# A two-block convolution kernel: first half image loaded in two parts, stores moved, ScalarE reordered around the second norm

## Chip, cores and metric

One core of one Trainium2 chip. The time is device microseconds of one execution of the whole program. The engines run their own instruction streams: TensorE (PE), VectorE (DVE), ScalarE (ACT), GpSimd (POOL) and SyncE (SP), which here only issues DMAs.

## What is computed

Four images of 64x64 pixels with 16 channels pass through two blocks, all in float32:

```python
# block 0
h  = layernorm(x) @ w_te + b_te                      # 16 -> 32
F  = fft2(h); fr = concat(real(F), imag(F))
fc = gelu(fr @ w_fc + b_fc)
x1 = x + real(ifft2(fc)) @ w_tp + b_tp
h2 = layernorm(x1) @ w_fe + b_fe                     # the "second norm"
d  = gelu(depthwise_conv3x3(h2) + b_dw)
x2 = x1 + d @ w_fp + b_fp
# block 1
qkv = conv3x3(layernorm(x2) @ w_hidden, w_qkv)       # 192 outputs: q, k, v
o   = irfft2(rfft2(q) * rfft2(k)) on 8x8 patches
out = (v * layernorm(o)) @ w_out + x2
```

## The kernel before

The program is one block in which each engine has a hand-written order, tied together by semaphores. The four images form two groups g = 0, 1 of two images each (128 partitions = 2 images x 64 rows). A norm has a number k (0, 1, 2) and runs per group and half: `centre` and `spread` on VectorE, `square` on ScalarE (L588), `variance` on VectorE (L787), `deviation` (square root) on ScalarE (L593), `normalise` on VectorE (L792, L793). k = 1 is the norm ahead of the depthwise convolution, k = 2 the one ahead of block 1.

Depthwise stage: for each group TensorE transposes four `windows` (L1157) of zp into banks 0 to 3; an eviction `w_evac` (L339) brings each into `uw`; `depthwise(j)` is three matmuls, each of two instructions (L1175), into bank 4 + j % 4; ScalarE applies Gelu with the bias (L677); `project(j)` (L1183) writes bank j; VectorE adds to x1 (L881), which gives x2. j runs over 0 to 7, four per group. ScalarE loads another function table whenever it changes between square root and Gelu (`load_table`, L582), but plain copies go with either.

Between the blocks the normed x2 is transposed (`channel_major`, L1192), scaled into `tr` with a border (`bordered`, L807), and split into three bf16 parts in `tr9` (`part` on ScalarE, L602 and L605; `split` on VectorE, L800 and L802). SyncE stores both to scratch tensors in DRAM: `store_padded(b)` (L445, three DMAs) and `store_parts(b)` (L452, six DMAs; for image 0 the last three are issued by ScalarE, L674). It then loads them back shifted, as the image of 9 taps: `load_taps` (L463, float32, 128 rows x 8 slots, each 4 x 66 - 2 = 262 elements) and `load_last` (L472, the same in bf16, 524 B each); together they are a "chunk", half an image in six DMAs. There are eight chunks; `arena` has room for four, and a buffer of the second group's is loaded when its four steps n have been gathered.

Block 1 runs 32 steps n, four per chunk. VectorE (`gather`) and ScalarE (`gather9`), both L378, lay out two tiles; TensorE runs `conv(n)` (L1229, 12 recorded instructions) into banks 0 and 1, ScalarE copies it out (`conv_out`, L709), then come `forward(n-1)` (L1240), ScalarE's `k_out` (L716), VectorE's `product` (L916) and `inverse(n-2)` (L1250) into bank 4 or 5. `forward(m)` waits for `product(m-1)`. For steps 0 and 1 of this loop group 1's last norm and `channel_major(1)` are still to be done. `keep_warm(times, a, free)` (L996) issues matmuls whose result is not used, into bank `free`; each gives two recorded instructions.

At the end `turn_weighted` (L1274), for i = 14 and 15, waits for VectorE's scaling (L937) of each, then come the last two output projections `unit` (L1286).

## Time and profile before

| | us |
|---|---|
| median of 3 runs (lowest to highest) | 236.66 (236.47 to 239.24) |
| the profiled execution | 237.58 |
| its span | 235.8 |
| TensorE busy | 219.5 (93%) |
| VectorE busy | 159.4 (68%) |
| ScalarE busy | 133.8 (57%) |
| GpSimd busy | 76.9 (33%) |

The span runs from the first to the last recorded instruction; the rest of an execution's time lies around it. Of the chain of work that ended last, 68% is TensorE's, 16% VectorE's, 6% ScalarE's and 6% DMA's. The stages: up to about 44 us load, first norm and the spectral part, to 56 the inverse transforms, to 94 the depthwise stage, and from 100 the 32 steps of block 1. A group of a timeline merges neighbouring instructions of one kind; the time in brackets is the engine's idle time before them and what ended it. Matmuls are pipelined, so merged TensorE groups overlap a little.

### The profile page before, as it was taken

Reading aid. Unit: us, or ns where it says so; the run is one execution under the profiler, and the core shown is the slowest. Engines: PE = TensorE matmul, PEld = TensorE weight load, DVE = VectorE, ACT = ScalarE, POOL = GpSimd, SP = SyncE. Lnnn points to the kernel's source line nnn. Section 1 sums busy time; section 2 is a strip of 40 time slices with the busy share of each in tenths; the row PEclk is TensorE's granted clock in tenths of the full one; section 3 lists DMA queues with packets and bytes.
Section 4 is the critical chain, followed back from the end, with each engine's and each line's share of the span. In section 5 each row is a group of like instructions: output and inputs, shape, how many; then the busy total and the mean of one; then the engine's idle time right before and its main releaser. Section 6 shows DMA issues by size and latency. Waiting matters only on the chain.

```text
span 235.8 us, 4977 instructions
## 1 busy us (share of the span) xinstructions
PE 219.5 (93%) x1926; PEld 144.1 (61%) x1926; DVE 159.4 (68%) x301; ACT 133.8 (57%) x286; POOL 76.9 (33%) x70
## 2 busy tenths in 40 slices
PE   7989999895989899779999999999999999999983
PEld 3359434772447557268676676767676777767561
DVE  3995123567743983646489978678786889677793
ACT  3366475323174754344678666667667576766533
POOL 1635500012300000000051766426654364549730
PEclk9999999999799999999999999999999999999999
DMA  6920000000000018989997479999950000000001
GB/s 215 329 70 7 16 8 4 20 3 0 4 0 0 0 64 190 223 193 194 201 197 151 141 137 191 182 179 202 191 118 0 3 24 25 0 1 3 22 0 67
DMA packets 22647, 21.07 MB, mean 89 GB/s; under 512 B 1898, under 2 KB 21242, under 8 KB 22522
## 3 DMA queue, kind: packets, MB, share of 16 engines
q1 hardware_dynamic: 22352, 20.62, 43.0%
q8 instruction: 15, 0.25, 0.5%
q10 hardware_dynamic: 272, 0.14, 0.3%
q14 instruction: 8, 0.07, 0.1%
HBM read 16.58 MB, written 4.02 MB: 87 GB/s over the span
## 4 chain that ended last, share of the span: by engine, by line
PE 68%; DVE 16%; ACT 6%; DMA 6%; issue 2%; SPq 1%; DVEq 0%; ACTq 0%
PE psum L1229 22%; PE psum L1240 13%; PE psum L1250 7%; PE psum L1102 5%; PE psum L1175 4%; PE psum L1260 3%; DMA arena<-parts 3%; DVE xc L781 2%; PE psum L1080 2%; DVE sq L793 2%; PE psum L1090 2%; PE psum L1063 2%; DMA parts<-tr 2%; DVE st L787 2%; PE psum L1286 2%
## 5 line engine op out<-in xcount | busy, mean ns | idle before, releaser
L1229 PE MATMUL psum<-wc,tile 128*128 128x192 f32 (+1 forms) x384 | 59.4, 305 | 3.5 <-ACT tile L378 1.9
L1229 PEld LDWEIGHTS psum<-wc,tile 128*128 128x128 f32 (+1 forms) x384 | 51.4, 159 | 13.7 <-issue 7.8
L557 POOL TENSOR_TENSOR zp<-zp,ln 128x512 f32<-128x512 f32 x14 | 17.8, 1274 | 100.6 <-DVE zp L937 100.6
L916 DVE TENSOR_TENSOR arena<-psum,arena 128x512 f32<-128x512 f32 x32 | 22.1, 691 | 27.5 <-ACT arena L716 27.2
L378 DVE COPY tile<-arena 128x256 f32<-128x256 f32 x64 | 25.1, 435 | 2.1 <-DMA arena<-parts 2.1
L1175 PE MATMUL psum<-arena,wdw 102*128 102x512 f32 x48 | 23.5, 631 | 0.9 <-ACT arena L339 0.9
L716 ACT COPY arena<-psum 128x512 f32<-128x512 f32 x32 | 18.8, 586 | 9.0 <-PE psum L1240 9.0
L1250 PE MATMUL psum<-arena,km 128*64 128x256 f32 x128 | 20.9, 405 | 0.2 <-DVE arena L916 0.2
L709 ACT COPY spec<-psum 128x768 f32<-128x768 f32 x16 | 12.8, 799 | 12.7 <-PE psum L1229 12.7
L558 POOL TENSOR_TENSOR zp<-zp,ln 128x512 f32<-128x512 f32 x14 | 17.8, 1271 | 1.1
L1240 PE MATMUL psum<-spec,km 64*128 64x256 f32 x128 | 18.2, 402 | 0.0
L378 ACT COPY tile<-arena 128x128 f32<-128x128 f32 x64 | 16.7, 314 | 2.4 <-DMA arena<-parts 2.4
L588 ACT ACTIVATE sq<-xc 128x512 f32<-128x512 f32 x12 | 7.7, 640 | 14.6 <-DVE xc L781 14.6
L646 ACT ACTIVATE arena<-psum,wt 128x512 f32<-128x512 f32 (+1 forms) x20 | 10.6, 614 | 9.0 <-PE psum L1102 9.0
L1175 PEld LDWEIGHTS psum<-arena,wdw 102*128 102x128 f32 x48 | 8.8, 196 | 9.9 <-issue 9.1
L1240 PEld LDWEIGHTS psum<-spec,km 64*128 64x128 f32 x128 | 11.0, 186 | 3.2 <-issue 2.5
L1250 PEld LDWEIGHTS psum<-arena,km 128*64 128x64 f32 x128 | 6.3, 134 | 10.8 <-issue 10.1
L926 DVE SCALAR_TENSOR_TENSOR zp<-stat,psum 128x512 f32<-128x512 f32 x16 | 11.0, 687 | 1.7 <-DVE stat L920 0.5
L703 ACT COPY arena<-psum 128x512 f32<-128x512 f32 x16 | 9.4, 590 | 4.5 <-PE psum L1274 3.5
L996 PE MATMUL psum<-arena 128*128 128x512 f32 x16 | 10.4, 807 | 1.4 <-POOL arena L509 1.4
L832 DVE COPY spec<-psum 128x512 f32<-128x512 f32 (+1 forms) x5 | 3.0, 596 | 12.6 <-PE psum L1090 12.6
L937 DVE TENSOR_TENSOR zp<-zp,stat 128x512 f32<-128x512 f32 x16 | 11.1, 692 | 0.5
(129 smaller groups left out, 373.1 us busy)
## 6 DMA issues: line engine op xcount, KB each, us to landing
arena<-padded SPq DMA_DIRECT2D x16, 393.0 KB, 9.8
arena<-parts SPq DMA_DIRECT2D x16, 196.5 KB, 9.7
arena<-padded SPq DMA_DIRECT2D x8, 262.0 KB, 10.4
parts<-tr SPq DMA_DIRECT2D x12, 115.5 KB
wq<-w_qkv SPq DMA_DIRECT2D x1, 1296.0 KB, 11.9
padded<-tr SPq DMA_DIRECT2D x4, 264.0 KB, 3.9
arena<-parts SPq DMA_DIRECT2D x8, 131.0 KB, 9.6
out<-xt SPq DMA_DIRECT2D x8, 128.0 KB, 1.7
```

The costliest lines, as they stand in the source:

```text
L378: o = copy(dst[:, n % 2, 2 * h:2 * h + 2].rearrange("p a (q x y) -> p (a q) x y", q=2, x=8), a)
L557: pool_link(pool.tensor_tensor(y, y, along(0), ALU.mult))
L558: pool_link(pool.tensor_tensor(y, y, along(1), ALU.add))
L709: act.copy(qkv[n // 2 % 4][:, n % 2].rearrange("p (a t) c -> p a (t c)", a=2), psum[:, 0:1024].rearrange("p (a n) -> p a n", a=2)[:, :, 0: ...
L716: act.copy(kh[:, m % 2], f_half(m, 1)).then_inc(k_ev, 1)
L916: dve.tensor_tensor(pr[:, m % 2], f_half(m, 0), kh[:, m % 2], ALU.mult).then_inc(prod, 1)
L937: dve.tensor_tensor(y, y, per_group(s[:, 3, :]), ALU.mult).then_inc(signal, 1)
L1102: last = mm(mix_bank(n, turn)[:, 0:w], wmix1[rows, b].rearrange("p s n -> p (s n)"), sp[rows, spans(n)], start=(n > 0 and not again), stop ...
L1175: last = mm(bank[4 + t4][:, :], wdw[:, dy].rearrange("p x h -> p (x h)"), uw[0:KW, 4 * t4:4 * t4 + 4, 2 * g:2 * g + 2, dy:dy + S], start=( ...
L1229: last = mm(bank[a][:, HID * h:HID * h + HID], stationary[:, n % 2, 2 * h + a, :], moving[:, :], start=first and h == 0, stop=not first, s ...
L1240: last = mm(f_banks(m)[q][:, 256 * part:256 * part + 256], const(name)[rows], qkv[m // 2 % 4][rows, m % 2, :, CH * part:CH * part + CH], s ...
L1250: last = mm(o_bank(i)[64 * q:64 * q + 64, 256 * e:256 * e + 256], const("inv4"), pr[:, m % 2, q, :], start=True, stop=True)
```

## The change

In program order of the diff:

- the first chunk is loaded in two parts, of two tap rows t each (rows of 130 elements), with a semaphore `im_first` for the first; gathers n = 0 and n = 2 wait for a part each
- SyncE stores the padded form of both images of group 0 first, then its share of image 0's parts, and then loads; the stores of image 1's parts are issued by ScalarE, all six ahead of Gelu(7)
- ScalarE's order around norm 1: deviation of half 0 ahead of the square of half 1; one eviction instead of two ahead of each square of group 1; the Gelu table is loaded ahead of evictions 2 and 3
- variance, deviation and normalise of group 1 in norm 2 move behind the first gathers (n = 0 and n = 1), `bordered(1)` to n = 2, `channel_major(1)` behind `inverse(0)`
- conv(0) writes banks 4 and 5, waits for x2_done 6, and conv(1) no longer waits for its copy; inverse(0) waits for x2_done 8
- keep_warm gives four matmuls instead of five ahead of conv(0), and one instead of two at the end.

```diff
--- before.py
+++ after.py
@@ -296,6 +296,7 @@
         st_dma = [sem(f"st_dma{b}") for b in range(NB)]
         st9_dma = [sem(f"st9_dma{b}") for b in range(NB)]
         part_act, part_dve = sem("part_act"), sem("part_dve")
+        im_first = sem("im_first")
         im_ld = [[sem(f"im_ld{b2}{th}") for th in range(2)] for b2 in range(2)]
         tiled, qkv_mm, qkv_ev = sem("tiled"), sem("qkv_mm"), sem("qkv_ev")
         f_mm, k_ev, prod, o_mm = sem("f_mm"), sem("k_ev"), sem("prod"), sem("o_mm")
@@ -368,7 +369,11 @@
 
         def chunk_landed(engine, n):
             g, th, b2, _, _ = where(n)
-            if n % 4 == 0:
+            if n == 0:
+                engine.wait_ge(im_first, 16 * CHUNK_LOADS)
+            elif n == 2:
+                engine.wait_ge(im_ld[0][0], 16 * CHUNK_LOADS)
+            elif n % 4 == 0:
                 engine.wait_ge(im_ld[b2][th], 16 * CHUNK_LOADS * (g + 1))
 
         def gather_into(copy, dst, src, e, n):
@@ -391,6 +396,9 @@
 
         def o_bank(i):
             return bank[4 + i % 2]
+
+        def conv_base(n):
+            return 4 if n == 0 else 0
 
         def f_banks(m):
             return (bank[2], bank[3]) if m < 31 else (bank[0], bank[1])
@@ -452,8 +460,7 @@
                         sp_.dma_start(parts[b, s0 - 2:s1 - 2, i], tr9[C * lane:C * (lane + s1 - s0), b % 2, i, t0:t0 + 8, :]
                                       .rearrange("p t y -> p (t y)")).then_inc(st9_dma[b], 16)
 
-            def load_taps(b, th, done):
-                t0, t1 = 4 * th, 4 * th + 4
+            def load_taps(b, t0, t1, done):
                 at, w = S2 * t0, S2 * (t1 - t0) - 2
                 sp_.wait_ge(st_dma[b], 16 * PAD_STORES)
                 slots = padded.rearrange("s c b n -> (s c) b n")
@@ -462,8 +469,7 @@
                     src = bass.AP(padded.tensor, slots[0:1, b, dy + at:dy + at + w].offset, [[NB * 8 * S2, n], [C * NB * 8 * S2, 8], [1, w]])
                     sp_.dma_start(dst, src).then_inc(done, 16)
 
-            def load_last(b, th, done):
-                t0, t1 = 4 * th, 4 * th + 4
+            def load_last(b, t0, t1, done):
                 at, w = S2 * t0, S2 * (t1 - t0) - 2
                 sp_.wait_ge(st9_dma[b], 16 * PART_STORES)
                 rows = parts[b].rearrange("s i c n -> (i c) s n")
@@ -473,14 +479,15 @@
 
 
             def load_chunk(g, th, b2):
-                load_taps(2 * g + b2, th, im_ld[b2][th])
-                load_last(2 * g + b2, th, im_ld[b2][th])
-
-            store_padded(0)
+                load_taps(2 * g + b2, 4 * th, 4 * th + 4, im_ld[b2][th])
+                load_last(2 * g + b2, 4 * th, 4 * th + 4, im_ld[b2][th])
+
+            for b in range(2):
+                store_padded(b)
             store_parts(0)
-            load_chunk(0, 0, 0)
-            store_padded(1)
-            store_parts(1)
+            for p, done in enumerate((im_first, im_ld[0][0])):
+                load_taps(0, 2 * p, 2 * p + 2, done)
+                load_last(0, 2 * p, 2 * p + 2, done)
             sp_.wait_ge(fp_mm, 8)
             load_chunk(0, 0, 1)
             for b2 in range(2):
@@ -603,6 +610,13 @@
                 else:
                     act.wait_ge(part_dve, 4 * g + b2 + 1)
                     act.copy(part_of(1, b2), left_of(g, b2)).then_inc(part_act, 1)
+
+            def store_parts(b, lanes):
+                act.wait_ge(part_dve, parts_ready(b))
+                for s0, s1, lane, t0 in lanes:
+                    for i in range(3):
+                        act.dma_start(parts[b, s0 - 2:s1 - 2, i], tr9[C * lane:C * (lane + s1 - s0), b, i, t0:t0 + 8, :]
+                                      .rearrange("p t y -> p (t y)")).then_inc(st9_dma[b], 16)
 
             act.wait_ge(ready0, 2)
             load_table(ACT.Sqrt)
@@ -650,17 +664,22 @@
                     square(1, 0, (0,))
                 act.wait_ge(i1_mm, j + 1)
                 act.copy(yy[:, j].rearrange("p q x -> p (q x)"), bank[j][:, :]).then_inc(i1_act, 1)
+            deviation(1, 0, (0,))
             square(1, 0, (1,))
-            deviation(1, 0)
+            deviation(1, 0, (1,))
             act.wait_ge(m2_mm, 5)
             for h in range(2):
-                for j in (2 * h, 2 * h + 1):
-                    act.wait_ge(w_mm, j + 1)
-                    w_evac(act.copy, j).then_inc(w_act, 1)
+                act.wait_ge(w_mm, h + 1)
+                w_evac(act.copy, h).then_inc(w_act, 1)
                 square(1, 1, (h,))
             deviation(1, 1)
+            load_table(ACT.Gelu)
+            for j in (2, 3):
+                act.wait_ge(w_mm, j + 1)
+                w_evac(act.copy, j).then_inc(w_act, 1)
             for g in range(G2):
-                load_table(ACT.Gelu)
+                if g == 1:
+                    load_table(ACT.Gelu)
                 for j in range(4 * g, 4 * g + 4):
                     if j == 5:
                         part(0, 0, 0)
@@ -668,11 +687,9 @@
                         part(0, 1, 0)
                     if j == 6:
                         part(0, 1, 1)
-                        s0, s1, lane, t0 = LANES[1]
-                        act.wait_ge(part_dve, parts_ready(0))
-                        for i in range(3):
-                            act.dma_start(parts[0, s0 - 2:s1 - 2, i], tr9[C * lane:C * (lane + s1 - s0), 0, i, t0:t0 + 8, :]
-                                          .rearrange("p t y -> p (t y)")).then_inc(st9_dma[0], 16)
+                        store_parts(0, LANES[1:])
+                    if j == 7:
+                        store_parts(1, LANES)
                     act.wait_ge(dw_mm, j + 1)
                     act.activation(gd_of(j), bank[4 + j % 4][:, :].rearrange("p (t b y) -> p t b y", t=4, b=2),
                                    ACT.Gelu, bias=vec("b_dw")).then_inc(gelu2, 1)
@@ -683,7 +700,8 @@
                         act.wait_ge(w_mm, j + 1)
                         w_evac(act.copy, j).then_inc(w_act, 1)
                 square(2, g, (1,))
-                deviation(2, g)
+                if g == 0:
+                    deviation(2, 0)
 
 
             def gather9(n):
@@ -707,7 +725,7 @@
                 if n >= 8:
                     act.wait_ge(gated, n // 2 - 3)
                 act.copy(qkv[n // 2 % 4][:, n % 2].rearrange("p (a t) c -> p a (t c)", a=2),
-                         psum[:, 0:1024].rearrange("p (a n) -> p a n", a=2)[:, :, 0:2 * HID]).then_inc(qkv_ev, 1)
+                         psum[:, 512 * conv_base(n):512 * conv_base(n) + 1024].rearrange("p (a n) -> p a n", a=2)[:, :, 0:2 * HID]).then_inc(qkv_ev, 1)
 
             def k_out(m):
                 act.wait_ge(f_mm, m + 1)
@@ -740,6 +758,8 @@
                 if n % 2 == 0 and n >= 8:
                     turned((n - 8) // 2)
                 conv_out(n)
+                if n == 0:
+                    deviation(2, 1)
                 if n >= 1:
                     k_out(n - 1)
                 if n % 2 == 0 and n >= 4:
@@ -883,8 +903,8 @@
                     if j % 2 == 1:
                         dve.wait_ge(x2_done, j + 1)
                         centre(g, t4 // 2, x2)
-                variance(2, g)
                 if g == 0:
+                    variance(2, 0)
                     normalise(2, 0, xc[:, 0])
                     dve.wait_ge(tr_zero, 1)
                     bordered(0)
@@ -956,12 +976,14 @@
                 if n + 1 < 32:
                     gather(n + 1)
                 if n == 0:
+                    variance(2, 1)
+                if n == 1:
                     normalise(2, 1, xc[:, 1])
                 if n % 2 == 1 and n >= 5:
                     o_scale((n - 5) // 2, o_norm)
                 if n >= 1:
                     product(n - 1)
-                if n == 1:
+                if n == 2:
                     bordered(1)
                 if n % 2 == 0 and n >= 4:
                     o_variance((n - 4) // 2)
@@ -1212,7 +1234,7 @@
             depthwise(7)
             for j in range(5, 8):
                 project(j)
-            keep_warm(5, km, 2)
+            keep_warm(4, km, 2)
 
 
             pe.wait_ge(tr_ev, 2)
@@ -1221,12 +1243,14 @@
             def conv(n):
                 pe.wait_ge(tiled, n + 1)
                 pe.wait_ge(tiled9, n + 1)
-                if n >= 1:
+                if n == 0:
+                    pe.wait_ge(x2_done, 6)
+                if n >= 2:
                     pe.wait_ge(qkv_ev, n)
                 for first, stationary, moving in ((True, tile, wc), (False, tile9_bf, wc9)):
                     for a in range(2):
                         for h in range(2):
-                            last = mm(bank[a][:, HID * h:HID * h + HID], stationary[:, n % 2, 2 * h + a, :], moving[:, :],
+                            last = mm(bank[conv_base(n) + a][:, HID * h:HID * h + HID], stationary[:, n % 2, 2 * h + a, :], moving[:, :],
                                       start=first and h == 0, stop=not first, skip_group_check=True)
                 last.then_inc(qkv_mm, 1)
 
@@ -1244,6 +1268,8 @@
             def inverse(m):
                 i, e = divmod(m, 2)
                 pe.wait_ge(prod, m + 1)
+                if m == 0:
+                    pe.wait_ge(x2_done, 8)
                 if e == 0 and i >= 2:
                     pe.wait_ge(o_centred, i - 1)
                 for q in range(2):
@@ -1290,11 +1316,10 @@
                 conv(n)
                 if n >= 1:
                     forward(n - 1)
-                if n == 1:
-                    pe.wait_ge(x2_done, 8)
-                    channel_major(1)
                 if n >= 2:
                     inverse(n - 2)
+                if n == 2:
+                    channel_major(1)
                 if n % 2 == 1 and 7 <= n < 31:
                     turn((n - 7) // 2)
                 u = unit_after((n - 8) // 2)
@@ -1308,7 +1333,7 @@
             turn(13)
             turn_bias(14)
             turn_bias(15)
-            keep_warm(2, km, 3)
+            keep_warm(1, km, 3)
             turn_weighted(14)
             turn_weighted(15)
             unit(6)
```

## Rows read from the trace of the kernel before

**Rows 1.** Windows: length, busy us of PE, PEld, DVE, ACT, POOL, then PEclk, DMA, GB/s

```profile
58.30:61.70 3.40, 3.40 (x5) 1.30 (x6) 3.30 (x6) 0.00 (x0) 0.91 (x1) 0.54 0.03 7
...
150.00:235.80 85.80, 81.04 (x596) 56.67 (x596) 64.53 (x128) 52.87 (x116) 43.62 (x34) 1.00 0.35 65
```

**Rows 2.** Timeline of ScalarE, second norm: start, busy, instruction [idle before]

```profile
55.12 0.30 ACT L593 ACTIVATE st<-st,eps 128x32 f32<-128x32 f32 x1
...
57.46 0.58 ACT L339 COPY arena<-psum 96x512 f32<-96x512 f32 x1
...
68.20 1.28 ACT L582 ACT_TABLE_LOAD   x1
```

**Rows 3.** Timeline of VectorE around the second norm

```profile
53.87 0.68 DVE L781 SCALAR_TENSOR_TENSOR xc<-st,x 128x512 f32<-128x512 f32 x1
...
55.91 0.69 DVE L793 TENSOR_TENSOR zp<-xc,st 128x512 f32<-128x512 f32 x1
...
62.07 0.69 DVE L781 SCALAR_TENSOR_TENSOR xc<-st,x 128x512 f32<-128x512 f32 x1
```

**Rows 4.** Timeline of TensorE in the depthwise stage

```profile
58.30 3.46 PE L1175 MATMUL psum<-arena,wdw 102*128 102x512 f32 x4 [0.93 <-ACT arena L339]
...
70.33 1.13 PE L1183 MATMUL psum<-wt,arena 128*128 128x96 f32 x8 [0.98 <-ACT arena L677]
...
71.30 2.77 PE L1175 MATMUL psum<-arena,wdw 102*128 102x512 f32 x6
```

**Rows 5.** Timeline of SyncE's DMA queue around the first loads

```profile
89.39 2.07 SPq L463 DMA_DIRECT2D arena<-padded  x3
...
92.80 1.33 SPq L472 DMA_DIRECT2D arena<-parts  x3
```

**Rows 6.** Timeline of VectorE before and at the first gathers

```profile
95.84 0.69 DVE L781 SCALAR_TENSOR_TENSOR xc<-st,x 128x512 f32<-128x512 f32 x1
...
99.73 0.90 DVE L378 COPY tile<-arena 128x256 f32<-128x256 f32 x4 [1.81 <-DMA arena<-parts]
...
111.59 0.50 DVE L378 COPY tile<-arena 128x256 f32<-128x256 f32 x2 [0.25 <-DMA arena<-parts]
```

**Rows 7.** Timeline of TensorE from the warm matmuls to conv(4)

```profile
94.14 4.48 PE L996 MATMUL psum<-km 128*128 128x512 f32 x10
...
100.48 1.87 PE L1229 MATMUL psum<-wc,tile 128*128 128x192 f32 x12 [1.86 <-ACT tile L378]
...
103.33 1.87 PE L1229 MATMUL psum<-wc,tile 128*128 128x192 f32 x12 [0.98 <-ACT spec L709]
...
113.97 1.90 PE L1229 MATMUL psum<-wc,tile 128*128 128x192 f32 x12
```

**Rows 8.** DMA packets in 93:94, 97:98, 112:113 us; then two windows

```profile
DMA packets 226, 0.23 MB, mean 227 GB/s; under 512 B 9, under 2 KB 226, under 8 KB 226
...
DMA packets 430, 0.22 MB, mean 221 GB/s; under 512 B 20, under 2 KB 426, under 8 KB 430
...
DMA packets 154, 0.15 MB, mean 151 GB/s; under 512 B 10, under 2 KB 154, under 8 KB 154
...
90.70:99.20 8.50, 7.92 (x37) 4.70 (x35) 5.13 (x9) 4.04 (x7) 0.00 (x0) 1.00 1.09 225
...
95.00:105.00 10.00, 7.16 (x33) 4.54 (x31) 5.96 (x15) 3.49 (x11) 0.00 (x0) 1.00 0.96 203
```

**Rows 9.** Issues of two lines on two queues: durations ns min/median/max

```profile
L452 SPq DMA_DIRECT2D parts<-tr x21: 407/749/877, 86.9 to 137.0; - x21
...
L674 ACTq DMA_DIRECT2D parts<-tr x3: 319/438/442, 86.9 to 87.7; - x3
```

**Rows 10.** Timeline of ScalarE, the last Gelu of the depthwise stage

```profile
91.69 0.69 ACT L677 ACTIVATE arena<-psum,wt 128x512 f32<-128x512 f32 x1 [2.78 <-PE psum L1175]
```

**Rows 11.** Timelines of TensorE and VectorE at the end

```profile
227.24 1.88 PE L996 MATMUL psum<-km 128*128 128x512 f32 x4
...
229.00 0.69 DVE L937 TENSOR_TENSOR zp<-zp,stat 128x512 f32<-128x512 f32 x1
```

## The prediction

> **What bounds the kernel now.** I read the chain of work that ended last first, then the timelines of TensorE, ScalarE, VectorE and SyncE around each place the diff touches, then the windows and the DMA traffic. From 150 us to the end TensorE is busy 81.0 of 85.8 us and most of what is missing lies in the last microseconds [rows 1], so a microsecond won before that comes through to the end, and one won on another engine doesn't. TensorE stood still where the diff works: 0.93 us before the first depthwise matmul, 0.98 us before the first projection [rows 4], 1.86 us before conv(0) and 0.98 us before conv(1) [rows 7]. All times below are in the coordinates of the profile of before; what an earlier stage wins is added at the end. The profiled execution has a span of 235.8 us and a time of 237.58; the median of the runs is 236.66. I take the gain off the median.
>
> **Part A, ScalarE around the second norm.** Before, deviation(1,0,first half) ran at 55.12, behind a square that waits for the centring at 53.87 to 54.55 [rows 2, 3], although its variance was ready at 53.9. Moved ahead it ends at about 54.3 and VectorE can normalise as soon as the centring ends: reciprocal from 54.6, product from 54.97 in place of 55.91 [rows 3], 0.94 us earlier. The second half follows: its deviation ends at 56.6, and the first eviction (L339) behind it starts at 56.6 and not 57.46 [rows 2], so the first depthwise matmul starts at 57.4 and not 58.30 [rows 4]. TensorE has only four short transposes (L1157) to do in between, which fit.
>
> The second gain is the table load. Before, ScalarE did evictions 2 and 3, the last square, two deviations, and only then the Gelu table (68.20) [rows 2] and the first Gelu (L677), for which TensorE waited 0.98 us [rows 4]. Now the last square follows the centring of 62.07 to 62.76 [rows 3], which is 0.94 earlier, so ends at 62.5; the variances and deviations end at 63.4; the table load of 1.28 us and its small activation end at 65.0; evictions 2 and 3 run to 65.5 and 66.0, the first Gelu to 66.7. Depthwise(2) now waits for eviction 2, that is 65.5, and takes 2.65 us (depthwise(3), six matmuls, filled 71.30 to 73.9 [rows 4]), to 68.2. The projection starts there in place of 70.33: **2.1 us**. From 70.3 to 94.1 TensorE has no long idle time before and keeps its order, so the whole stage moves.
>
> The granted clock was 0.54 between 58.30 and 61.70 [rows 1], the lower of the two levels, 1.2 GHz, for most of it, and it fell just after the wait of 0.93 us [rows 4]. Four depthwise matmuls took 3.46 us there [rows 4], of which full clock would give back half. With the clock up depthwise(2) would still wait for eviction 2 at 65.5, with the clock down TensorE arrives at 65.6. So I count nothing for the clock: 2.1 us either way, bounds 1.7 and 2.2. The Trainium skill ("TensorE: Matmul & The Clock Gate", Part 1) says that K is binary, full or half rate; the trace agrees, and its 0.54 is a mix of the two.
>
> **Part B, the first half image.** Before: load_taps(0) is issued at 89.39, its last-tap loads at 92.80 because they wait for the stores of the parts [rows 5], and all has landed when VectorE starts its first gather at 99.73 [rows 6]; conv(0) follows at 100.48 [rows 7]. A chunk is 1024 rows of 1048 B and 1024 of 524 B, 1.61 MB. Rows of 1048 B went at 226 packets per us (227 GB/s), rows of 524 B at 430 (221 GB/s) [rows 8]: bytes bound both. All data together, padded(1)'s store among it, ran at 225 GB/s between 90.7 and 99.2; later, with slow heads of a load in it (154 packets per us), at 203 from 95 to 105 [rows 8]. I use 213 between them.
>
> After: the first part is 1024 rows of 520 B and 1024 of 260 B, 0.80 MB. At 213 GB/s that is 3.75 us. No row shows packets of 260 B in number. Lower bound: the same byte rate, 1.2 us for 1024. Upper bound of the nearest row: the same 430 packets per us as 524 B, 2.4 us. I take the middle, 0.6 us over the byte rate, for the sum and keep both ends. Ahead of them now run the stores of parts(1), six DMAs of 0.40 MB on ScalarE's queue, 1.85 us at the same rate. So: 90.7 + 1.85 + 3.75 + 0.6 + 0.5 (last data to landing, as 99.2 to 99.7) = 97.4. The loads of the last taps can't be issued before 92.8 either (their store is where it was; the second padded store is issued while SyncE waited for part_dve anyway), and the data of the taps and of parts(1) fills the time until 95, so this wait is covered. VectorE is free at 96.53 [rows 6], since variance(2,1) now comes behind the gathers; TensorE's four warm matmuls of 0.9 us end at 97.7 in place of five at 98.6 [rows 7]. So the load ends last: conv(0) at 97.4 + 0.75 = 98.15 (before: 99.73 to 100.48). Bounds 97.8 (warm matmuls) and 99.3.
>
> ScalarE's six issues come before Gelu(7). They start at 88.9, and by SyncE's median 0.75 us for a large one and ScalarE's 0.44 for a small one [rows 9] take 3 x 0.75 + 3 x 0.44 = 3.6 us, to 92.5. Gelu(7) was at 91.69 [rows 10], so it is 0.9 us late. Cover: TensorE is busy with projections 5 and 6 until 93.25 (the warm matmuls start at 94.14 [rows 7] and project(7) before them takes 0.9), and Gelu(7) ends at 93.2. Without that cover every microsecond more delays project(7), the warm matmuls and VectorE's last x2.
>
> Conv(1) has banks of its own and no wait for the copy of conv(0): its 0.98 us of idle goes [rows 7]. From conv(0) to conv(4) before were 113.97 - 100.48 = 13.5 us [rows 7], now 12.5: conv(4) at 110.65. Two things are late next. Part two of the chunk lands at 96.9 + 3.75 + 0.6 + 0.5 = 101.75, and conv(2), due at 98.15 + 4.75 = 102.9, needs 0.75 for its gathers: 0.4 us to spare. Behind this gather on VectorE lie normalise(2,1) (2.0 us) and product(0) (0.7), for which forward(1) waits; they end at 104.9, when it is due at 104.7: 0.1 to 0.2 us lost. And the second chunk (image 1), before ready at 111.59 [rows 6]: it wins 1.6 us (0.33 MB of padded(1) are stored earlier, in idle DMA time), about 1.0 us of the half-empty time behind the old stores, and loses up to 2.4 us for short rows, so 109 to 111.4, and conv(4) wants it at 110.0. Part B: 113.97 - 110.75 = **3.2 us**, bounds 1.7 and 3.6.
>
> The other moves (variance, deviation and normalise of group 1, channel_major(1) behind inverse(0)) shift the same instructions into gaps of VectorE's waits for DMA and k; the waits for x2_done 6 and 8 were met by 95.1. At nothing.
>
> **Part C, the end.** One warm matmul pair instead of two leaves at 228.3, not 229.1. The first turn can start then, the second waits for VectorE's last scaling, 229.00 + 0.69 [rows 11], and takes 0.9 us, to 230.6 in place of 230.9: **0.3 us**, bounds 0 and 0.3.
>
> **Sum.** 2.1 + 3.2 + 0.3 = 5.6 us; 236.66 - 5.6 = 231.1. The bounds together: 3.4 to 6.1, 230.5 to 233.3.
>
> **Rivals.**
> 1. Short rows cost twice. The sum has 1.85 us for 1024 rows of 260 B (1.25 by bytes and 0.6). If they took 4.8 us, half the rate of the 524 B rows, each part would land 2.95 us later: part two at 107.65, conv(2) at 108.4, conv(4) 12.5 - 4.75 = 7.75 us later at 116.15, 2.2 later than before. 2.1 - 2.2 + 0.3 = 0.2, time 236.5. For it: the trace has no such rows; against it: 524 B rows lost nothing against 1048 B. Chance 0.10. The Trainium skill ("DMA: Bandwidth & Descriptors", Specifications) gives 512 B as the least transfer for line rate, with a read-modify-write below; that speaks against this change, and by it the time would be this rival's 236.5; no run so far shows it.
> 2. The other side: the short rows go at the lowest packet rate of the trace, 154 per us [rows 8], 6.6 us for 1024. Twice 4.75 us more puts part two at 111.25, conv(2) at 112.0 and conv(4) at 119.75, 5.8 later than before; with 2.1 and 0.3 won the kernel would be 3.4 us slower, 240.1. The sign turns at conv(4) at 116.4, about 4.9 us per 1024 rows. Against it: those 154 are a short dip at the head of each load. Chance 0.03.
> 3. ScalarE is held by its issues, 1 us each (SyncE's longest was 0.88 [rows 9]), while SyncE issues too. Gelu(7) ends at 95.6, project(7) at 96.5, the four warm matmuls at 100.1, conv(0) at 100.2 and conv(4) at 112.7: Part B shrinks to 1.3, time 233.0. Chance 0.12.
> 4. Part A gives only its first 0.9 us, because an eviction or a deviation stands in the new order behind something late (the table load before evictions 2 and 3, above all). 0.9 + 3.2 + 0.3 = 4.4, time 232.3. Chance 0.13.
> 5. The change does not act: the first part is only ready when the whole was, as the stores of parts(1) and the second part share the engines with it. Then 0.98 + 2.1 + 0.3 remain, 233.3. Chance 0.08.
>
> **Numbers.** My forecast, with 229.7 to 232.6 around it, has 0.54. A measurement of this kernel can tell about 2%, here 4.7 us: under 231.9. The centre of the forecast is 0.8 past it. 0.44 of the forecast's 0.54, 0.05 of rival 4's 0.13 (its own spread reaches below) and 0.06 of rivals 3 and 5 lie there: faster 0.55; slower 0.02 (240.1 is not yet over 2%, the worst of rival 2 is); within 2% the rest, 0.43. The range for 8 in 10 is 229.6 to 234.8: it takes in rivals 3, 4 and 5 and leaves out 1 and 2.
>
> **What would show it.** First depthwise matmul 0.9 us earlier, the wait of L1183 for ScalarE gone and a short one of L1175 for L339 instead, project(0) at 68.2. Then, less 2.1: first gather at 97.4, four warm matmuls and under 1 us idle before conv(0), none before conv(1), conv(4) at 110.7. Wrong if TensorE waits for project(7), if packets under 512 B go at well under 400 per us, or if conv(2) or conv(4) waits for a gather over 0.5 us.

## The result, and the profile after

| | before | after |
|---|---|---|
| median of 20 runs each (lowest to highest) | 237.44 (235.69 to 240.12) | 235.64 (234.57 to 238.93) |
| ratio | 1 | 0.9932 (0.9903 to 0.996) |
| the profiled execution | 237.58 | 236.54 |
| its span | 235.8 | 234.7 |
| its mean granted clock | 0.993 | 1.0 |

The kernel is 0.7% faster by the ratio, 1.6 us, and 1.8 us by the medians, where 5.6 us were forecast; 235.64 lies outside the range of 229.6 to 234.8. The two spans differ by 1.1 us. Ratios, here and below, leave out executions over 1.5% above the fastest of their kernel, medians do not, so the two can differ.

The first group below is TensorE's timeline of the kernel after (start us, busy us, instruction, idle before and what ended it). It answers to [rows 4, 7, 11].

```profile
53.86 1.96 PE L1163 MATMUL psum<-arena,km 128*128 128x512 f32 x4 [0.80 <-ACT arena L666]
...
57.96 1.96 PE L1197 MATMUL psum<-arena,wdw 102*128 102x512 f32 x4 [0.93 <-ACT arena L340]
...
66.21 2.84 PE L1197 MATMUL psum<-arena,wdw 102*128 102x512 f32 x6 [0.92 <-ACT arena L340]
68.89 1.03 PE L1205 MATMUL psum<-wt,arena 128*128 128x96 f32 x8
...
92.77 1.13 PE L1205 MATMUL psum<-wt,arena 128*128 128x96 f32 x8 [0.91 <-ACT arena L694]
93.74 3.62 PE L1018 MATMUL psum<-km 128*128 128x512 f32 x8
99.07 3.53 PE L1253 MATMUL psum<-wc,tile 128*128 128x192 f32 x24 [1.71 <-ACT tile L383]
...
104.32 1.87 PE L1253 MATMUL psum<-wc,tile 128*128 128x192 f32 x12 [0.66 <-ACT spec L727]
...
112.92 1.87 PE L1253 MATMUL psum<-wc,tile 128*128 128x192 f32 x12 [0.73 <-ACT spec L727]
...
228.67 1.16 PE L1300 MATMUL psum<-km,zp 128*128 128x128 f32 x8 [0.41 <-DVE zp L957]
```

project(0) starts at 68.89 instead of 70.33: 1.44 us won, not 2.1. From there to conv(0) it is 30.18 us, and 30.15 before; to conv(4) it is 44.03 against 43.64. So all that this execution won in Part A is kept, and Part B gave 0.39 us back where 3.2 were to be won. From conv(4) to the end of the span it is 121.8 us in both, and 121.8 to 121.9 in all other profiles of this study but one (stores on SyncE, 123.5, where the clock falls at conv(4)): what is won before conv(4) reaches the end, and nothing is won behind it. The windows of the same kernel (length, busy PE, PEld, DVE, ACT, POOL, then clock, DMA share, GB/s), to be read against [rows 1]:

```profile
58.30:61.70 3.40, 3.04 (x11) 1.26 (x10) 3.30 (x6) 1.10 (x2) 1.13 (x1) 1.00 0.03 7
150.00:234.70 84.70, 79.55 (x586) 55.58 (x586) 64.69 (x127) 52.09 (x115) 42.89 (x34) 1.00 0.36 65
```

The clock is 1.00 (2.4 GHz) in the stretch where before had 0.54. TensorE is still all but full from 150 us on, so what is won earlier does reach the end.

ScalarE's timeline and its DMA queue (ACTq), then VectorE's, of after [rows 2, 3, 6, 10]:

```profile
53.95 0.32 ACT L600 ACTIVATE st<-st,eps 128x32 f32<-128x32 f32 x1 [0.24 <-DVE st L807]
...
57.13 0.57 ACT L340 COPY arena<-psum 96x512 f32<-96x512 f32 x1
...
64.19 1.28 ACT L589 ACT_TABLE_LOAD   x1
...
65.59 1.05 ACT L340 COPY arena<-psum 96x512 f32<-96x512 f32 x2
...
86.67 5.31 ACTq L618 DMA_DIRECT2D parts<-tr  x6
92.03 0.69 ACT L694 ACTIVATE arena<-psum,wt 128x512 f32<-128x512 f32 x1 [4.68 <-issue]
```

```profile
53.83 0.68 DVE L801 SCALAR_TENSOR_TENSOR xc<-st,x 128x512 f32<-128x512 f32 x1
...
54.81 1.46 DVE L813 TENSOR_TENSOR zp<-xc,st 128x512 f32<-128x512 f32 x1
...
98.29 0.90 DVE L383 COPY tile<-arena 128x256 f32<-128x256 f32 x4 [2.48 <-DMA arena<-parts]
...
102.95 0.50 DVE L383 COPY tile<-arena 128x256 f32<-128x256 f32 x2 [2.57 <-DMA arena<-parts]
...
111.55 0.49 DVE L383 COPY tile<-arena 128x256 f32<-128x256 f32 x2 [1.46 <-DMA arena<-parts]
```

The deviation left its old place (55.12 to 53.95), but the product that it frees (L813) now takes 1.46 us and not 0.69, and evictions 2 and 3 stand at 65.59. In the second group the first gather is at 98.29, 12.98 us after the first store of parts was issued at 85.31; before, it was 12.86 [rows 6, 9]. The second chunk's gather, at 111.55, is where it was in before, at 111.59.

conv(4) waits for this chunk by way of ScalarE, whose order is its own gather of step 4 first and the copy of conv(3) behind it:

```profile
111.55 0.53 ACT L383 COPY tile<-arena 128x128 f32<-128x128 f32 x2 [3.62 <-DMA arena<-parts]
111.98 0.79 ACT L727 COPY spec<-psum 128x768 f32<-128x768 f32 x1
```

TensorE is released by the second of them ("ACT spec L727" in its row at 112.92), 1.37 us after the chunk has landed.

SyncE's queue of after, where the loads begin [rows 5], and from the chain of waits the store for which they wait, in before and then in after:

```profile
85.31 2.47 SPq L460 DMA_DIRECT2D parts<-tr  x3
87.82 3.31 SPq L470 DMA_DIRECT2D arena<-padded  x3
92.67 1.34 SPq L478 DMA_DIRECT2D arena<-parts  x3
```

```profile
88.60 4.18 DMA parts<-tr
...
87.04 5.61 DMA parts<-tr
```

Counted from the first store of parts, the loads of the last taps leave at +7.36 us; before, at +5.93. The transfer on which they wait took 5.61 us; before, 4.18.

**One thing comes ahead of all comparisons: the level of the clock.** Each execution carries a mean granted clock, and the times sort by it. Over all comparisons of this study but the one above, for which the clocks of before are not on record, the kernel before has 81 executions: 28 at 0.996 or more with a median of 236.51 us, 42 between 0.99 and 0.996 with a median of 238.1, and 11 below that with 240.1. Of the kernel after, 16 of 20 have 0.996 or more, with a median of 235.22. At a full clock the change is therefore worth about 1.3 us, and some 0.5 us more comes from lower stretches that no longer happen (the medians of the table above lie 0.93 and 0.42 above those at full clock). One execution of before (1172 us) and one of the late addition (415.6 us) stand far off; the first is left out, the second is in its kernel's median (234.17 without it) and not in its value at full clock. I use this split below: "at full clock" means the executions at 0.996 or more.

### The profile page after: what moved, and what is told of

Same layout as the page of the kernel before. It is cut to its first block, busy times and chain, and to the rows that moved or that the text cites. A ratio compares the mean times of both kernels' runs of the same rounds, so it can differ in the third digit from the quotient of the medians.

```text
span 234.7 us, 4977 instructions
## 1 busy us (share of the span) xinstructions
PE 216.4 (92%) x1922; PEld 142.8 (61%) x1922; DVE 160.4 (68%) x301; ACT 133.6 (57%) x286; POOL 77.0 (33%) x70
## 4 chain that ended last, share of the span: by engine, by line
PE 59%; DVE 15%; DMA 12%; SPq 5%; ACT 4%; issue 3%; DVEq 0%; ACTq 0%
PE psum L1253 19%; PE psum L1264 12%; PE psum L1276 6%; DMA wq<-w_qkv 5%; PE psum L1124 5%; DMA arena<-parts 4%; PE psum L1286 3%; DMA parts<-tr 2%; PE psum L1197 2%; PE psum L1102 2%; PE psum L1112 2%; PE psum L1085 2%; PE psum L1312 2%; SPq L478 2%; SPq L470 2%
## 5 line engine op out<-in xcount | busy, mean ns | idle before, releaser
L936 DVE TENSOR_TENSOR arena<-psum,arena 128x512 f32<-128x512 f32 x32 | 22.1, 691 | 22.8 <-ACT arena L734 22.6
L383 DVE COPY tile<-arena 128x256 f32<-128x256 f32 x64 | 25.6, 442 | 6.5 <-DMA arena<-parts 6.5
L1197 PE MATMUL psum<-arena,wdw 102*128 102x512 f32 x48 | 22.4, 599 | 2.2 <-ACT arena L340 2.2
L727 ACT COPY spec<-psum 128x768 f32<-128x768 f32 x16 | 12.8, 799 | 10.2 <-PE psum L1253 10.2
L565 POOL TENSOR_TENSOR zp<-zp,ln 128x512 f32<-128x512 f32 x14 | 17.8, 1273 | 1.1
L660 ACT ACTIVATE arena<-psum,wt 128x512 f32<-128x512 f32 (+1 forms) x20 | 10.6, 614 | 9.0 <-PE psum L1124 9.0
L901 DVE TENSOR_TENSOR x<-psum,x 128x256 f32<-128x256 f32 x8 | 3.3, 422 | 12.0 <-PE psum L1205 12.0
```

What stands on the lines that cost most here:

```text
L383: o = copy(dst[:, n % 2, 2 * h:2 * h + 2].rearrange("p a (q x y) -> p (a q) x y", q=2, x=8), a)
L565: pool_link(pool.tensor_tensor(y, y, along(1), ALU.add))
L727: act.copy(qkv[n // 2 % 4][:, n % 2].rearrange("p (a t) c -> p a (t c)", a=2), psum[:, 512 * conv_base(n):512 * conv_base(n) + 1024].rearr ...
L936: dve.tensor_tensor(pr[:, m % 2], f_half(m, 0), kh[:, m % 2], ALU.mult).then_inc(prod, 1)
L1197: last = mm(bank[4 + t4][:, :], wdw[:, dy].rearrange("p x h -> p (x h)"), uw[0:KW, 4 * t4:4 * t4 + 4, 2 * g:2 * g + 2, dy:dy + S], start=( ...
```

## The experiments

Stage lengths below are differences of starts in one profile: **stage A** from the last inverse transform (53.86 in after) to project(0); **gather** from the issue of the first store of parts to VectorE's first gather; **stage B** from project(0) to conv(4). What they are in the kernels of this study:

| kernel | stage A | gather | stage B | median us | at full clock |
|---|---|---|---|---|---|
| before, two profiles | 16.46, 16.34 | 12.86, 13.09 | 43.64, 43.86 | 237.44 | 236.51 (28 of 81) |
| before + two warm pairs | 14.72 | 13.69 | 45.95 | 238.72 | 236.3 (4 of 10) |
| before + Part A | 15.05 | 13.07 | 43.74 | 236.54 | 236.23 (6 of 10) |
| after, two profiles | 15.03, 15.04 | 12.98, 12.51 | 44.03, 42.87 | 235.64 | 235.22 (16 of 20) |
| after, stores on SyncE | 15.03 | 10.58 | 43.20 | 237.12 | 234.66 (3 of 10) |
| after, whole first chunk | 15.05 | 16.07 | 48.24 | 241.24 | none of 4 |
| late x1 addition, twice | 14.26, 14.25 | 12.29, 11.99 | 42.34, 42.30 | 234.22, 234.72 | 234.2, 233.95 |
| + old loads and stores | 14.28 | 13.74 | 46.25 | 236.79 | 234.32 (3 of 10) |
| + old loads, 8 warm pairs | 14.27 | 13.70 | 43.19 | 235.06 | 235.06 (4 of 4) |
| + taps of both parts first | 14.27 | 14.67 | 45.72 | 237.56 | 236.12 (1 of 10) |
| + stores behind Gelu(7) | 14.29 | 11.29 | 42.80 | 235.14 | 235.06 (5 of 6) |
| + both of these | 14.27 | 15.37 | 46.78 | 238.95 | none of 10 |
| + third order | 14.28 | 13.03 | 44.11 | 235.88 | 235.3 (3 of 10) |
| + conv(0) in banks 0, 1 | 14.26 | 12.56 | 43.52 | 234.81 | 234.81 (4 of 4) |
| + five warm pairs | 14.26 | 12.12 | 42.94 | 235.02 | 235.02 (4 of 4) |
| + Gelu table between evictions | 13.08 | 11.90 | 42.24 | 234.02 | 234.02 (6 of 6) |

Rows that begin with a "+" are edits on top of the late addition.

**What ends stage B.** In the profiles with the loads in two parts in which conv(4) waits for the second chunk, stage B is the time from the first store of parts to that chunk's gather, plus 17.8 us (16.4 from project(0) to that store, and 1.37 from the chunk to conv(4)): 26.24 and 44.03 in after, 25.08 and 42.87 in its second profile, 24.52 and 42.30 in the late addition, 25.15 and 42.94 with five warm pairs, 25.01 and 42.80 with the stores behind Gelu(7), 25.74 and 43.52 with the old banks, 25.40 and 43.20 with the stores on SyncE. The start of conv(0) does not enter: there it lies between 27.8 and 30.2 us after project(0). Before and Part A alone have 24.72 and 25.07 to that gather, and 43.64 and 43.74: there TensorE's own chain is longer than the landing. So the new loads make TensorE ready sooner and bring the chunk for which it then waits no earlier.

### Part A alone

```diff
+            deviation(1, 0, (0,))
             square(1, 0, (1,))
-            deviation(1, 0)
+            deviation(1, 0, (1,))
...
+            load_table(ACT.Gelu)
+            for j in (2, 3):
+                act.wait_ge(w_mm, j + 1)
+                w_evac(act.copy, j).then_inc(w_act, 1)
```

> The kernel before with only ScalarE's new order around the second norm (Part A). Theory 1 (Part A is worth what the changed kernel shows in its own stage and passes through): project(0) at 68.9 in place of 70.3, everything behind it 1.4 us earlier, conv(0) at 99.0, conv(4) at 112.5, time 1.4 us under before, so as fast as the whole change. Rival (the loads are limited by something that doesn't move with the stage): conv(4) stays within 0.4 us of 113.97 and the time gains under 0.5 us.

Ratio 1.0 (0.995 to 1.0049). Its stage A is after's (15.05), its stage B before's (43.74). Its median is 236.54 where before had 237.83 beside it: six of its ten executions are at full clock, against 8 of before's 19. At full clock it takes 236.23, 0.3 below before's 236.51, which the spread of before's executions (235.91 to 237.97) doesn't tell from nothing. So the 1.4 us expected are in the profile and in the medians, where before has its fall of the clock, and not where the clock is up. None of its ten executions reads 0.993, the value of the two profiles of before with the fall at 58.6 us; its other four read 0.983 to 0.992.

### Is it the clock that before lost at 58.6 us?

The kernel before with one warm pair ahead of the first four short transposes and one behind them; nothing else is changed. A second profile of before itself ran beside it.

```diff
+            keep_warm(1, km, 3)
             windows(0, (0,))
+            keep_warm(1, km, 3)
```

> The kernel before with one warm matmul ahead of and one behind the first four transposes of the depthwise stage (0.9 us each, in the two waits there). Theory: the clock does not fall near 58.6 us; depthwise(0) starts at 58.3 as before or up to 0.4 later, project(0) at 68.7 to 69.3, the stretch is gone from all executions, and the time is that of the full-clock executions of the kernel before, 236.5 (ratio 0.993 to 0.996). Rival (the stretch costs nothing, as my prediction had it): ratio 1.00, project(0) at 70.3.

> The kernel before once more, unchanged, for a second profile. Theory (Part A mostly gives back what a stretch at 1.2 GHz costs): in an execution without that stretch project(0) is at 68.7 to 69.2 and not 70.3, so Part A is worth 0 to 0.5 us at full clock. Rival (Part A's order is worth 1.4 us by itself): project(0) at 70.3 also at full clock.

TensorE's timeline of the kernel with the warm pairs, where before has [rows 4]:

```profile
56.54 1.96 PE L1141 MATMUL psum<-arena,km 128*128 128x512 f32 x4 [0.80 <-ACT arena L652]
...
60.92 1.96 PE L1175 MATMUL psum<-arena,wdw 102*128 102x512 f32 x4
...
71.26 1.13 PE L1183 MATMUL psum<-wt,arena 128*128 128x96 f32 x8 [0.98 <-ACT arena L677]
```

The four depthwise matmuls take 1.96 us and not 3.46 [rows 4], and stage A is 14.72 us with the old order of ScalarE. The second profile of before has the lower clock at the same place again (3.06 us for the four, stage A 16.34). The old order at full clock is thus 1.7 us shorter than before's profile showed, and no longer than the new one (15.03). The expected time (236.5) was missed: the median is 238.72 and the ratio 1.0003 (0.9951 to 1.0056). Four of ten executions are at full clock, with a median of 236.3, and five at 0.984 or less, with 239.3; in the profiled one the clock was down from 16 to 20 us and again from 102 to 106, at conv(0). The warm pairs cure the place, not the kernel, and why the clock falls elsewhere more often stays open.

### GpSimd's addition beside the normalisation

```diff
+                    if g == 0 and h == 1:
+                        pool.wait_ge(z_done, half_no(1, 0, 0))
```

> The changed kernel, but GpSimd's second addition to x1 waits until VectorE has made the first normalised half. Theory (in the change the product of the first half took 1.46 us and not 0.69 because GpSimd's addition runs beside it): the product takes 0.69 again, the first eviction starts 0.7 to 0.8 us earlier at 56.4, depthwise at 57.2, project(0) at 68.2. Rival (1.46 us has another cause): 1.46 stays and nothing moves.

> The changed kernel with GpSimd's late addition once more, unchanged, in more rounds. Theory: 14.3 us from the second inverse transform to project(0), median 234.2 to 234.9, ratio 0.985 to 0.989. Rival (the first timing was lucky): 0.993 as the changed kernel.

GpSimd's second addition to x1 ran from 54.59 to 55.72, beside VectorE's first product of the norm. Here it waits for that product. The product in this kernel:

```profile
55.01 0.69 DVE L815 TENSOR_TENSOR zp<-xc,st 128x512 f32<-128x512 f32 x1
```

0.69 us again. Stage A is 0.77 us shorter, which is the whole difference of 1.46 and 0.69, and the times are 234.22 and 234.72 in two comparisons: ratios 0.9862 (0.9807 to 0.9918) and 0.9891 (0.9828 to 0.9954). The Trainium skill ("SBUF — State Buffer", "SBUF: two separate sides") says that a VectorE instruction with two inputs in SBUF and a GpSimd operation that reads SBUF exclude each other for the whole of one of them. The trace agrees: the product's record begins at 54.81, just after the addition's, and ends 0.55 us after the addition, so most of its own 0.69 us lies behind it.

### The Gelu table between evictions 2 and 3

```diff
-            load_table(ACT.Gelu)
             for j in (2, 3):
                 act.wait_ge(w_mm, j + 1)
                 w_evac(act.copy, j).then_inc(w_act, 1)
+                if j == 2:
+                    load_table(ACT.Gelu)
```

This kernel has the late addition too.

> The changed kernel with GpSimd's late addition, and the Gelu table loaded between evictions 2 and 3, not ahead of both. Theory (the new order makes depthwise(2) wait 0.92 us for an eviction behind the table load, which at full clock costs as much as it saves): depthwise(2) waits 0.1 us or not at all, from the second inverse transform to project(0) 13.4 us in place of 14.3, time 0.5 to 0.9 us under the variant with the late addition alone, 0.982 to 0.984 of before. Rival (another wait follows, or the second chunk takes it up): stage shorter, time the same within 0.3 us.

ScalarE's timeline of this kernel, then TensorE's:

```profile
64.08 0.56 ACT L340 COPY arena<-psum 96x512 f32<-96x512 f32 x1
64.66 1.28 ACT L591 ACT_TABLE_LOAD   x1
...
66.06 0.56 ACT L340 COPY arena<-psum 96x512 f32<-96x512 f32 x1
```

```profile
64.28 3.60 PE L1200 MATMUL psum<-arena,wdw 102*128 102x512 f32 x8
67.71 1.03 PE L1208 MATMUL psum<-wt,arena 128*128 128x96 f32 x8
```

Eviction 2 runs at 64.08, TensorE no longer waits before depthwise(2) (0.92 us in after), and stage A is 13.08 us: 1.95 shorter than after's. The median is 234.02, ratio 0.987 (0.9811 to 0.9928), with a profiled span of 231.8. Against the late addition alone (234.22, 234.72; at full clock 234.2, 233.95) the times don't separate it, and the 0.982 to 0.984 expected was missed. The stage is 1.2 us shorter in the profile, but it also began later than in the two others (54.63 against 54.05 and 53.78), so the spans differ by only 0.3 to 0.7 us. That the 1.2 us reach the time isn't shown.

### Who delays the first part: the stores on ScalarE's queue

```diff
+            store_parts(1)
             sp_.wait_ge(fp_mm, 8)
...
-                    if j == 7:
-                        store_parts(1, LANES)
```

> The changed kernel, but the six stores of parts(1) are issued by SyncE behind both parts of the first chunk, as in the kernel before, and not by ScalarE. Theory 1 (these stores run into the landing of parts(0)): parts(0) lands about 4.2 us after its last issue in place of 5.6, the first last-tap load is issued at 91.3 and not 92.67, Gelu(7) is at 90.3, the first gather at about 96.5, conv(0) at 97.3; whether conv(4) gains depends on the second chunk, whose stores are now later. Rival (short rows are the cause): last-tap loads still at 92.6, first gather at 98.3.

VectorE's gathers of this kernel, then TensorE's conv(4):

```profile
96.35 0.90 DVE L383 COPY tile<-arena 128x256 f32<-128x256 f32 x4 [0.92 <-DMA arena<-parts]
...
111.17 0.50 DVE L383 COPY tile<-arena 128x256 f32<-128x256 f32 x2 [3.76 <-DMA arena<-parts]
```

```profile
112.53 2.58 PE L1252 MATMUL psum<-wc,tile 128*128 128x192 f32 x12 [3.03 <-ACT spec L726]
```

From its chain of waits, the store for which the last taps wait:

```profile
87.51 4.53 DMA parts<-tr
```

It takes 4.53 us and not 5.61, and the last taps leave at +6.29 us and not +7.36. The first gather comes 10.58 us after the first issue, 2.4 us earlier than in after and 1.9 earlier than in its second profile, and Gelu(7) is on time. conv(0) starts 27.80 us after project(0), as early as the prediction had it (98.15 - 70.33). But the second chunk, with those stores now ahead of it on SyncE, leaves VectorE waiting 3.76 us and TensorE 3.03, and conv(4) then takes 2.58 us and not 1.87, for the clock fell. Median 237.12, ratio 0.9976 (0.993 to 1.0022). So the stores cost the first part about 2 us where they are issued ahead of it, and the second chunk where they are issued ahead of that; and with conv(0) where it was foretold, stage B is still 43.20, because conv(4) waits for the chunk.

### The first chunk in one piece

```diff
-            for p, done in enumerate((im_first, im_ld[0][0])):
-                load_taps(0, 2 * p, 2 * p + 2, done)
-                load_last(0, 2 * p, 2 * p + 2, done)
+            load_chunk(0, 0, 0)
```

> The changed kernel with the first chunk loaded whole (rows of 1048 and 524 B) and not in two parts. Theory 1: last-tap loads are still issued at 92.6; first gather at 99.5 to 100, conv(0) 1.3 us later than with two parts, but the second chunk lands 0.5 to 1 us earlier than 111.5. Rival (short rows cost the DMA engines much): the second chunk lands 2 us or more earlier, 109.5, and the kernel is faster than the change by 1 us.

VectorE's first gather, then TensorE's first two convolutions:

```profile
101.64 0.90 DVE L378 COPY tile<-arena 128x256 f32<-128x256 f32 x4 [6.07 <-DMA arena<-parts]
```

```profile
102.42 6.19 PE L1246 MATMUL psum<-wc,tile 128*128 128x192 f32 x24 [5.30 <-ACT tile L378]
```

The gather falls back to 16.07 us, TensorE idles 5.30 us and the first two convolutions take 6.19 us instead of 3.53. 241.24, ratio 1.0173 (1.0134 to 1.0211). With the moved stores the two parts are worth 3.1 to 3.6 us to the first gather (against the two profiles of after) and, with the clock, 5.6 us in all. The second chunk landed about 24.3 us after the first store of parts (its last load issued at 99.3, landed 10.6 later), against 26.24 and 25.08 in after: earlier by 0.8 to 1.9 us, between the 0.5 to 1 of the theory and the 2 of the rival. What the two ways load between 89 and 109 us (traffic of after, then of this kernel):

```profile
DMA packets 7108, 3.87 MB, mean 194 GB/s; under 512 B 2411, under 2 KB 7108, under 8 KB 7108
```

```profile
DMA packets 5352, 4.24 MB, mean 212 GB/s; under 512 B 284, under 2 KB 5352, under 8 KB 5352
```

3.87 MB against 4.24 MB in the same 20 us, 194 and 212 GB/s. And two single microseconds of after in which the rows of 260 B go:

```profile
DMA packets 764, 0.24 MB, mean 243 GB/s; under 512 B 593, under 2 KB 764, under 8 KB 764
```

```profile
DMA packets 557, 0.18 MB, mean 178 GB/s; under 512 B 410, under 2 KB 557, under 8 KB 557
```

764 packets in one microsecond, far above the 430 of [rows 8], and 557 in another at a lower rate of bytes. Most of the 9% between the two kernels is not the short rows' doing: 0.28 of the 0.37 MB are missing between 89 and 95 us (204 against 250 GB/s), where the DMA engines of after were 80% busy and those of this kernel 95%, with half as much to load queued in after while SyncE waited for the store. From 95 to 103 us all are busy and half of after's packets are short (1605 of 3194, against 120 of 2156): 187 against 204 GB/s, which is 0.14 MB or 0.7 us. The Trainium skill ("DMA: Bandwidth & Descriptors", Specifications) wants 512 B for full rate, and by it the short rows were rival 1; the trace has a loss of at most 8% in that stretch, and not the half rate of rival 1.

### Old loads, with and without warm matmuls

Both on top of the late addition. The first takes loads and stores of before; the second adds eight warm pairs instead of four ahead of conv(0).

```diff
-            for b in range(2):
-                store_padded(b)
+            store_padded(0)
             store_parts(0)
-            for p, done in enumerate((im_first, im_ld[0][0])):
-                load_taps(0, 2 * p, 2 * p + 2, done)
-                load_last(0, 2 * p, 2 * p + 2, done)
+            load_chunk(0, 0, 0)
+            store_padded(1)
+            store_parts(1)
...
-                    if j == 7:
-                        store_parts(1, LANES)
```

and in the second kernel also

```diff
-            keep_warm(4, km, 2)
+            keep_warm(8, km, 2)
```

> Everything of the changed kernel (with GpSimd's late addition) but the loads and stores, which are those of the kernel before: one whole chunk, padded(1) and parts(1) behind it, all by SyncE. Theory (two parts and moved stores bring next to nothing, since the second chunk lands no earlier): second chunk 24.7 to 25.1 us after the parts' first issue, time within 0.5 us of the same kernel with the new loads, 0.986 of before. Rival (the new loads carry the gain of Part B): conv(0) 2 us later and the time 1.5 us or more longer.

> The kernel with the loads of before and the rest of the change, with eight warm matmuls ahead of conv(0) in place of four. Theory (with the old loads TensorE stands over 3 us, the granted clock falls to 0.5 for 3.4 or 6.8 us and half of that is lost, which is what the early first part saves): eight matmuls end about when the chunk lands, no stretch at the lower level, conv(4) 1.5 to 3 us earlier than without them, time 0.985 to 0.99 of before against 0.992. Rival (the clock is not what sets this variant's time): conv(4) within 0.5 us and the ratio stays.

TensorE of the first, then of the second:

```profile
91.85 3.63 PE L1012 MATMUL psum<-km 128*128 128x512 f32 x8
99.09 6.54 PE L1247 MATMUL psum<-wc,tile 128*128 128x192 f32 x24 [3.61 <-ACT tile L378]
```

```profile
91.83 7.06 PE L1012 MATMUL psum<-km 128*128 128x512 f32 x16
99.03 3.53 PE L1247 MATMUL psum<-wc,tile 128*128 128x192 f32 x24
```

The same data, landed at the same time. With four pairs TensorE idles 3.61 us, the clock falls and two convolutions take 6.54 us; with eight they take 3.53. The medians are 236.79 (0.9924, 0.9874 to 0.9974) and 235.06 (0.9889, 0.9861 to 0.9917). The times of the first are the rival's of its expectation and not the theory's: 2.1 to 2.6 us longer than the late addition. Seven of its ten executions are below full clock; its three others have 234.32, no more than the kernels with the new loads have (234.2, 233.95). By stage B the new loads are 0.85 us better (42.3 against 43.19), by the times between nothing and 0.9 (235.06 against 234.2 at the most). So with TensorE kept warm, loading in two parts and moving the stores is worth less than 1 us, and its larger use, the rest of the 2.1 to 2.6, is that TensorE has less time to idle in.

### Other orders of the same DMAs

Four more kernels, all on the late addition: taps of both parts ahead of the wait for the stores; ScalarE's stores behind Gelu(7); both of these; and a third order, in which SyncE takes taps, stores and the second part while ScalarE issues the last taps of the first.

```diff
-            for p, done in enumerate((im_first, im_ld[0][0])):
-                load_taps(0, 2 * p, 2 * p + 2, done)
-                load_last(0, 2 * p, 2 * p + 2, done)
+            halves = (im_first, im_ld[0][0])
+            for p in range(2):
+                load_taps(0, 2 * p, 2 * p + 2, halves[p])
+            for p in range(2):
+                load_last(0, 2 * p, 2 * p + 2, halves[p])
```

> The changed kernel with GpSimd's late addition, and SyncE issues the taps of both parts before it waits for the stores of parts(0), then the last taps of both. Theory 1 (the DMA engines stand half idle while SyncE waits for that landing, and the second chunk is what conv(4) waits for): DMA share before the last taps rises from 0.76 to 1; the first gather comes 0 to 1 us later, the second part and the second chunk 1 to 2 us earlier; no wait before conv(4); time equal to or up to 0.5 us under the variant without this order. Rival (the second chunk is bound by bytes from 94 us on, nothing is won by filling the hole): second chunk lands at the same distance from the parts' first issue, 24.4 to 26.2 us.

The same two rows of this kernel:

```profile
99.25 0.90 DVE L383 COPY tile<-arena 128x256 f32<-128x256 f32 x4 [4.17 <-DMA arena<-parts]
```

```profile
100.03 5.08 PE L1257 MATMUL psum<-wc,tile 128*128 128x192 f32 x24 [3.40 <-ACT tile L383]
```

The taps of the second part fill the time in which SyncE waited, and delay the first: gather 14.67, TensorE idle for 3.40, clock down. 237.56 (0.9984, 0.9948 to 1.0019), where 0 to 1 us of delay and an equal time were expected. The second chunk then needs no wait at all, since TensorE is late.

```diff
-                    if j == 7:
-                        store_parts(1, LANES)
...
+                if g == 1:
+                    store_parts(1, LANES)
```

> The changed kernel with GpSimd's late addition, and ScalarE issues the six stores of parts(1) behind Gelu(7). Theory 1 (issued before it they slow SyncE's own issues, hold Gelu(7) and delay the landing of parts(0)): parts(0) lands 6.0 to 6.3 us after its first issue and not 7.2 to 7.4, no wait before project(7), first gather 10.6 to 11 us after that issue and not 12.3 to 13; conv(4) not earlier than the second chunk, which lands as late as before the edit; time within 0.5 us of the variant without it. Rival (the stores cost by their bytes wherever they stand): first gather still at 12 us or more.

Gelu(7) at 89.90, project(7) without a wait, last taps issued at +5.92 us, as in before, gather 11.29, 0.7 to 1.0 us earlier than in the late addition. The second part lands no earlier (gather 16.5 us after the first issue, against 16.75 and 16.48), and the second chunk 0.5 us later (25.0 against 24.4 and 24.5); VectorE waits 3.14 and 1.36 us for them. Stage B 42.80, 235.14 (0.9879, 0.9838 to 0.992): no better than the late addition alone.

> Both edits together: stores of parts(1) behind Gelu(7), taps of both parts ahead of the wait. Theory 1: parts(0) lands in 6.0 to 6.3 us, the taps are in by then, first gather at 10.6 to 11.5 us, second chunk at 23 to 24 us, conv(4) without a wait: 0.5 to 1.5 us under the better of the two alone. Rival (bytes bind): second chunk at 24.4 us or later, no gain over either.

Both together: gather 15.37, TensorE idle for 5.25, 238.95 (1.0052, 1.0022 to 1.0082), where 0.5 to 1.5 us were to be won. The third order:

```diff
-            for p, done in enumerate((im_first, im_ld[0][0])):
-                load_taps(0, 2 * p, 2 * p + 2, done)
-                load_last(0, 2 * p, 2 * p + 2, done)
+            load_taps(0, 0, 2, im_first)
+            load_taps(0, 2, 4, im_ld[0][0])
+            store_parts(1)
+            load_last(0, 2, 4, im_ld[0][0])
...
-                    if j == 7:
-                        store_parts(1, LANES)
...
+                if g == 1:
+                    act.wait_ge(st9_dma[0], 16 * PART_STORES)
...
+                        act.dma_start(dst[:, :, 0:2 * S2 - 2], taken[0:n, :, 2:2 * S2]).then_inc(im_first, 16)
```

> The changed kernel with GpSimd's late addition; SyncE issues the taps of both parts, the stores of parts(1) and the last taps of part two, ScalarE issues the last taps of part one behind Gelu(7). Theory (the first part was late because its last taps wait behind or beside other data, the hole before them was empty): first gather at 10.6 to 11.5 us after the parts' first issue, second part at 15, second chunk at 23, no wait before conv(2) and conv(4); 0.5 to 1.5 us under the variant with late addition alone (0.986 of before), so 0.980 to 0.984. Rival (bytes in front, on whichever queue, hold the first part): first gather at 13 us or later, clock falls, no gain.

Gather 13.03, TensorE idle for 2.90 with the clock down behind it, 235.88 (0.9922, 0.9878 to 0.9966): the rival of its expectation. No order brings both the first part and the second chunk early: each stands where the bytes ahead of it let it.

### Banks for conv(0), and one more warm pair

```diff
         def conv_base(n):
-            return 4 if n == 0 else 0
+            return 0
...
-                if n >= 2:
+                if n >= 1:
                     pe.wait_ge(qkv_ev, n)
```

> The changed kernel with GpSimd's late addition, but conv(0) in banks 0 and 1 and conv(1) waits for its copy, as before. Theory (what ends last is the landing of part two and of the second chunk, not the start of conv(1)): the wait of 0.98 us before conv(1) is back, but the waits before conv(2) and conv(4) take it up: conv(4) within 0.5 us, the ratio stays at 0.986 to 0.99. Rival (the 0.98 us counts in full, as in my sum): conv(4) and the time 1 us later.

The wait of 0.98 us before conv(1) is back. Stage B is 43.52 against 42.34 and 42.30, but here the second chunk also came later (25.74 us after the first issue, against 24.40), and conv(4) still waited 0.18 us for it: in this execution an earlier conv(1) would have won nothing. From conv(0) to conv(3) it is 10.12 us here and 9.47 and 9.50 in the late addition, where conv(2) waits 0.46 and 0.49 us for ScalarE and here not at all. So of the 0.98 us some 0.6 reach conv(3), and conv(4) gets of them what the second chunk's landing leaves. By the times 234.81 (0.9884, 0.9839 to 0.9928) can't be told from 234.22 and 234.72; the share in the time stays open.

```diff
-            keep_warm(4, km, 2)
+            keep_warm(5, km, 2)
```

> The changed kernel with GpSimd's late addition and five warm matmuls ahead of conv(0) in place of four. Theory (the fifth fits into the 1.4 us that TensorE waits there): conv(0) unchanged, no stretch at the lower clock, time equal to the variant with four (ratio 0.986), 1.5 us or more under the changed kernel at best. Rival (a fifth pushes conv(0) back): 0.5 us longer.

235.02 (0.9896, 0.9834 to 0.9959), at full clock 235.0 against 234.2 and 233.95. TensorE had 1.2 to 1.5 us to spare there, which one more pair fills; it gains nothing. The second profile of after ran beside these:

> The changed kernel once more, unchanged, for a second profile. Theory (the landing of the second chunk sets conv(4) and varies by 1 to 2 us between executions, as the times at full clock do, 234.6 to 236.5): conv(4) less project(0) is anywhere from 42.3 to 44.0 and the time moves with it. Rival (the time varies for another reason): conv(4) less project(0) at 44.0 again with another time.

235.99 us, stage A again 15.04, stage B 42.87: the second chunk came 1.2 us earlier than in the first profile, and conv(4) waited only about 0.1 us for it. The 0.73 us that TensorE waited for conv(4) in the first profile isn't there in each execution: the six profiles with after's loads and banks have 44.03, 42.87, 42.94, 42.34, 42.30 and 42.24, as the second chunk lands between 26.24 and 24.40 us after the first store of parts.

## Why the prediction was wrong

The sum was 2.1 + 3.2 + 0.3. At full clock the runs give 0.3 + 1.0 + 0.0: Part A alone takes 236.23 where before takes 236.51, and after 235.22. Two steps failed, one in each large part. With Part A alone at 0.3 the sum would give 232.9, with Part B alone at 1.0 it would give 233.3, both inside the range; only both together, and Part C at nothing, lead out of it, to 235.4.

**Part A, the first step: right in place, wrong in size.** The deviation and the reciprocal moved as foretold, but the first depthwise matmul came at 57.96, not 57.4. The term "VectorE normalises from 54.97" priced the product at the 0.69 of [rows 3]. That row is of an instruction that ran when GpSimd's addition was over; moved 1.1 us ahead, it ran beside it and took 1.46. The late addition gives the 0.77 back, and its stage A of 14.26 is the 14.3 that the prediction had for the new order (53.87 to 68.2).

**Part A, the table load: right in mechanism, a term missing.** Depthwise(2) waited for eviction 2, as said, 0.92 us, from 66.21 and not 65.5; the rest is the 0.77 us of the slow product, carried along. Rival 4 named this place and was half right: the wait is real, and it is lifted by one eviction moved ahead of the load (1.2 us).

**Part A, "I count nothing for the clock": this is the first step that failed.** For the new order it held: the wait for eviction 2 set the stage. For the old order it did not. With the clock up, before's own stage is 14.7 us (the run with warm pairs), the new one 15.0. What the profile shows as 1.44 us won is the fall of the clock that before had in this execution and after had not. By the stages Part A would lose 0.3 us at full clock, by the times it wins 0.3; both are too small to be told from nothing. Of before's executions about a third are at full clock, and the median of three that I subtracted from, 236.66, was by its times of that kind (236.47 and 236.66), while the profile from which the terms came, at 0.993 and 237.58, was of the other. I noted the gap of 0.9 us between them and did not ask what it was. The same clock row, 0.54, that I quoted, was the answer: a gain read off a profile at one level can't be taken off a median at the other.

**Part B, the second chunk: the second step that failed.** The forecast let it win 1.6 us, since padded(1) is stored in idle DMA time, and about 1.0 behind the old stores, and lose up to 2.4 for short rows: 109 to 111.4, which is 22.1 to 24.5 us after the first store of parts, with conv(4) 0.75 us behind it. It was gathered after 24.4 to 26.2 us in the profiles with after's loads, where the old loads have 24.7 to 25.2: nothing won. And conv(4) came 1.37 us behind it, since ScalarE's copy of conv(3) stands behind its gather (rows at 111.55 and 111.98). This wait ends last. The run with its stores on SyncE shows it: there conv(0) was as early as foretold, the chunk came after 25.4 us, inside the range of the others, and stage B was 43.20. Whether the copy of conv(3) ahead of that gather would win the 0.6 us between 1.37 and 0.75 was not tried.

**Part B, the first part of the image: "this wait is covered" failed too.** The last taps' loads weren't issued at 92.8 less the shift but 1.4 us later (+7.36 against +5.93; over all profiles 6.98 to 7.38 with after's loads, 5.75 to 6.35 with those of before), because the store that they wait for, of image 0, ran beside six stores of image 1: 5.61 us against 4.18, and 4.53 without those six. I had let the moved stores cost 1.85 us of bandwidth ahead of the loads and nothing on the store in flight. The run without them on ScalarE's queue puts their price at 1.9 to 2.4 us; the run with one piece puts the worth of the two parts at 3.1 to 3.6. The foretold 2.3 us (99.73 to 97.4) became 0.2 between before and after (means of two profiles each, 12.97 and 12.75), and 1.6 on the late addition (13.74 and 13.70 with the old loads, 12.29 and 11.99 with the new). Rival 5, "the first part is only ready when the whole was", is what the first profile showed.

**ScalarE's issues.** Three large and three small were to take 3.6 us; they took 5.31 (ACTq row at 86.67; 4.80 to 5.05 in four other profiles), while SyncE's three tap loads took 3.31 and not 2.07. So Gelu(7) was not 0.9 us late but held until 92.03, and project(7) waited 0.91 us. That is most of rival 3, and it cost nothing here, since conv(0) waited for the load anyway (1.71 us). Behind Gelu(7) the same six took 4.37. The Trainium skill ("DMA: Bandwidth & Descriptors", "Issuing engines are not separate DMA queues") says that several issuing engines share the same 16 engines and save only the time to issue; the trace agrees, and even that time was longer when both issued (5.31 against 4.37 us).

**Short rows.** Rivals 1 and 2 are out: 764 packets in a microsecond. What the short rows cost, at most 0.7 us for the 1605 of them from 95 to 103 us, is in the order of the 0.6 us per 1024 that the sum had. The second chunk, foretold at 109 to 111.4 in before's coordinates, was gathered at 111.55, which is 113.0 in them; in the second profile of after it is 111.8, in those with the late addition 111.2 to 111.9. How much of this is short rows, and how much the stores, no run separates. conv(2) and conv(4) waited 0.66 and 0.73 us in after.

**Conv(1) without a wait: right.** conv(0) and conv(1) merge into 3.53 us. Of the 0.98 us some 0.6 reach conv(3), and conv(4) only where the second chunk lands early enough (banks, above).

**Part C: 0.3 foretold, 0.0 measured.** Turn 15 waits 0.41 us for VectorE's last scaling (228.67), as the prediction had it, but then takes 1.16 us and not 0.9. From conv(4) to the end of the span it is 121.78 us with one warm pair (after), and 121.83 and 121.81 with two (before, Part A alone).

What stays open: why the clock falls in some executions and not in others of the same kernel, and what keeps the second chunk from landing earlier than with the old loads.

## What to carry to other kernels

Look at the mean granted clock of the profiled execution before its durations are used: if a stretch is at the lower level, find out whether the times that the forecast is set against have it too. A row's duration holds for its surroundings: if an instruction is moved, look at what the other engines do at the new time, GpSimd beside VectorE first. And a store whose landing a load waits for was late here by what else was in flight: transfers moved "into idle time" beside it came back as its lateness. Before an earlier start is counted, follow the next thing that is waited for: here conv(0) could come 2.4 us earlier and conv(4) still wait for the second chunk.

## What the runs showed of the hardware

- The same kernel is at full clock in one of three executions and below it in two (81 executions of before: medians 236.51, 238.1 and 240.1). The two profiled ones were at 0.993 and had one stretch at the lower clock, near 58.3 to 62.5 us.
- TensorE idle for 5.30, 5.25, 3.61, 3.40 and 2.90 us ahead of conv(0) was each time followed by a lower clock: 6.19, 5.43, 6.54, 5.08 and 5.12 us for two convolutions; idle for 2.68 us, by 3.35 us for one in place of 1.87, and for 3.03 us ahead of conv(4), by 2.58. With 0.35 to 1.71 us idle the two took 3.53, and with 1.86 and 2.09 the first took 1.87. At 58.3 us an idle time of only 0.92 to 0.93 did it for the old order, behind one of 0.92 ahead of the transposes; for the new order the same 0.93 did not, behind one of 0.60.
- VectorE's product of two SBUF tiles took 1.46 us beside GpSimd's addition, and 0.69 alone.
- A DMA issue took 0.88 us on average on ScalarE's queue when SyncE issued too (six in 5.31 us; 0.80 to 0.84 in four other profiles), 0.73 when they came behind Gelu(7) (4.37), 0.63 on SyncE in the old order (six in 3.8 us).
- Rows of 260 B: 764 packets in one microsecond, 557 in another; over 8 us with all DMA engines busy 187 GB/s where half of the packets are under 512 B, 204 GB/s where 6% are.
- TensorE's wait for a load can run through another engine: conv(4) started 1.37 us after the chunk had landed, behind ScalarE's gather (0.53) and copy (0.79).
